# Order of the row gathers, the turn of the next keys and the scaling of the probabilities in a four-layer kernel with paged attention

## The reference, cut to what matters

```python
k_blocks = k_blocks.at[blk, :, off, :].set(k.transpose(0, 2, 1, 3))
v_blocks = v_blocks.at[blk, :, off, :].set(v.transpose(0, 2, 1, 3))
k_all = k_blocks[block_tables].transpose(0, 2, 1, 3, 4).reshape(Bx, G, -1, HD)
v_all = v_blocks[block_tables].transpose(0, 2, 1, 3, 4).reshape(Bx, G, -1, HD)
scores = jnp.einsum('bghtd,bgsd->bghts', qg, k_all) * SCALE
allowed = (kpos[None, None, :] <= pos[:, :, None]) & (kpos[None, None, :] > pos[:, :, None] - WINDOW)
scores = jnp.where(allowed[:, None, None, :, :], scores, -jnp.inf)
p = jax.nn.softmax(scores, axis=-1)
o = jnp.einsum('bghts,bgsd->bghtd', p, v_all).reshape(Bx, H, Tx, HD)
x = x + jnp.einsum('bto,do->btd', o.transpose(0, 2, 1, 3).reshape(Bx, Tx, H * HD), Wo)
```

## Time and profile before

| | |
|---|---|
| median of 3 runs | 185.62 us (184.13 to 185.85) |
| profiled execution | 187.31 us, span 185.5 us |
| granted TensorE clock, mean | 0.844 |
| PE busy, instructions | 125.4 us, 1310 |
| DVE busy | 109.0 us, 404 |
| ACT busy | 77.2 us, 250 |
| POOL busy | 77.0 us, 104 |
| bytes moved | 31.72 MB, mean 171 GB/s |

### The profile page before, as it was taken

The page is one execution under the profiler, slowest core; times in us unless marked ns, Lnnn a source line. Parts: engine busy times, 40 slices in busy tenths (PEclk is TensorE's granted clock), DMA queues, the critical chain, the costliest instruction groups (busy, mean ns, idle before and its releaser), DMA issues.

```text
span 185.5 us, 4024 instructions
## 1 busy us (share of the span) xinstructions
PE 125.4 (68%) x1310; PEld 82.2 (44%) x1310; DVE 109.0 (59%) x404; ACT 77.2 (42%) x250; POOL 77.0 (41%) x104
## 2 busy tenths in 40 slices
PE   0222999910049899040537798988989898999974
PEld 0112955500037487030313343665656565656742
DVE  0886665000099986999111576675888887977220
ACT  0120210005963356992202347583836584763300
POOL 3277640120000123000877888889888740414000
PEclk9999999995557999955555555699999999999999
DMA  4978999999967777671233368852687765465662
GB/s 111 269 159 206 215 146 115 164 200 168 227 187 184 207 189 176 177 236 66 80 92 113 115 189 234 231 179 83 174 266 224 217 179 142 157 166 153 193 173 79
DMA packets 33536, 31.72 MB, mean 171 GB/s; under 512 B 6636, under 2 KB 31340, under 8 KB 32812
## 3 DMA queue, kind: packets, MB, share of 16 engines
q1 hardware_dynamic: 27090, 19.46, 37.7%
q0 software_dynamic: 3216, 11.15, 27.4%
q10 hardware_dynamic: 3210, 0.87, 2.4%
HBM read 23.47 MB, written 8.00 MB: 170 GB/s over the span
## 4 chain that ended last, share of the span: by engine, by line
PE 25%; DMA 20%; SPq 19%; POOL 18%; issue 8%; DVE 6%; ACT 2%; DVEq 0%; POOLq 0%
SPq L342 16%; DMA blk<-in_L_cond_k_blocks,tab_i 14%; POOL kvA L434 8%; PE bank L1157 5%; PE bank L1114 4%; PE bank L1098 4%; DMA kv_rows<-kvn 4%; PE bank L1144 4%; PE bank L1131 3%; SPq L347 3%; PE bank L1152 3%; POOL kvB L427 2%; DMA lens_i<-in_itok_B 2%; POOL tab_i L396 2%; POOL blkp L434 2%
## 5 line engine op out<-in xcount | busy, mean ns | idle before, releaser
L596 ACT ACTIVATE pr<-S,nb 128x160 f32<-128x160 f32 x64 | 26.9, 423 | 17.6 <-DVE nb L906 17.5
L1098 PE MATMUL bank<-KT,QT 32*64 32x160 f32 x256 | 22.5, 374 | 1.2 <-DVE nb L906 0.8
L897 DVE TENSOR_SCALAR pr<-pr,ri 128x128 f32<-128x128 f32 x64 | 21.8, 385 | 1.1
L1017 PE MATMUL bank<-WkvT,x2T 128*128 128x256 f32 x32 | 9.5, 463 | 16.7 <-DVE WqT L775 15.9
L906 DVE CUSTOM_DVE_ANT_0 S<-bank,mask 128x160 f32<-128x160 f32 x64 | 18.1, 319 | 4.5 <-PE bank L1098 4.1
L582 ACT COPY PTA<-bank 128x256 f32<-128x256 f32 x32 | 11.9, 373 | 12.9 <-PE bank L1114 12.8
L434 POOL DMA_INDIRECT kvA<-kv_rows,rowA x16 | 15.4, 961 | 4.5 <-issue 4.5
L434 POOL DMA_INDIRECT blkp<-kv_rows,rowA x16 | 15.7, 983 | 3.2 <-issue 3.0
L1017 PEld LDWEIGHTS bank<-WkvT,x2T 128*128 128x128 f32 x32 | 7.4, 239 | 19.6 <-issue 16.7
L423 POOL TENSOR_TENSOR ksn<-kvn,rot 128x512 f32<-128x512 f32 x2 | 3.5, 1772 | 30.0 <-DVE kvn L823 30.0
L881 DVE COPY KT<-bank 128x512 f32<-128x512 f32 x8 | 5.5, 690 | 16.2 <-PE bank L1076 16.1
(11 more groups left out here) (181 smaller groups left out, 278.1 us busy)
## 6 DMA issues: line engine op xcount, KB each, us to landing
We<-in_L_cond_W SPq DMA_DIRECT2D x16, 256.0 KB, 3.4
kvn<-in_L_cond_W SPq DMA_DIRECT2D x16, 256.0 KB, 3.8
kv_rows<-blkp SPq DMA_DIRECT2D x2, 968.0 KB
xin<-in_x SPq DMA_DIRECT2D x2, 512.0 KB, 8.1
kv_rows<-kvn SPq DMA_DIRECT2D x2, 512.0 KB, 8.3
be<-in_L_cond_b SPq DMA_DIRECT2D x32, 32.0 KB
out<-nat SPq DMA_DIRECT2D x8, 128.0 KB
kv_rows<-QT SPq DMA_DIRECT2D x1, 968.0 KB
```

Source lines behind the costliest of these rows:

```text
L596: act.activation(pr[:, n // B4 % 2, u, n % B4, :], S[:, n % 2, u, :], ACT.Exp, bias=nb[:, n % 4, u:u + 1], scale=-1.0, accum_out=rs[:, n % ...
L897: ts(e_, e_, ri[:, n % 8, u:u + 1], None, ALU.mult).then_inc(s_pn, 1)
L1017: i_ = mm(bank[1 + t // 2][:, (t % 2) * D:(t % 2) * D + D], x2T[:, kc, t * P:(t + 1) * P], WkvT[:, kc, :], start=(kc == 0), stop=(kc == KC ...
L1098: i_ = mm(bank[2 + i % 3][GS * T * k:GS * T * k + GS * T, 0:KEYS], QT[h, g, j, :], KT[h, g % 2, j, :], start=True, stop=True)
```

## The change

The order of the gathers changes, by this part of the diff:

```diff
+FIRST = 4
...
-            for b in range(AHEAD):
+            for b in range(FIRST):
                 gather_a(b)
+            pool.wait_ge(s_kt, 1)
+            nxt = FIRST
             pool.wait_ge(s_cst0, 16)
             for n in range(B + 2):
...
-                if n + AHEAD < B:
-                    gather_a(n + AHEAD)
+                while nxt < min(B, n + AHEAD, 2 * n + FIRST + 2):
+                    gather_a(nxt)
+                    nxt += 1
```

`s_kt` reaches 1 when TensorE has turned the first 128 keys of the first group. After step n the gathers of min(n+10, 2n+6) sequences have been issued; before it was n+11. The turn of the next group's keys stands one step later on TensorE, and so do both copies; each head pair's two products become one:

```diff
# scalar
-                if n % B4 == 1 and n // B4 + 1 < NT:
+                if n % B4 == 2 and n // B4 + 1 < NT:
                     keep_kb(n // B4 + 1)
# vector
-                for u in range(2):
-                    e_ = pr[:, n // B4 % 2, u, n % B4, 0:P]
-                    ts(e_, e_, ri[:, n % 8, u:u + 1], None, ALU.mult).then_inc(s_pn, 1)
+                e_ = pr[:, n // B4 % 2, :, n % B4, 0:P]
+                tt(e_, e_, ri[:, n % 8, :].unsqueeze(2).broadcast_to([P, 2, P]), ALU.mult).then_inc(s_pn, 1)
...
-                if n % B4 == 0 and n // B4 + 1 < NT:
+                if n % B4 == 1 and n // B4 + 1 < NT:
                     keep_k(n // B4 + 1)
# tensor
-                    pe.wait_ge(s_pn, 2 * (B4 * g + j))
+                    pe.wait_ge(s_pn, B4 * g + j)
...
-                if n % B4 == 0 and n // B4 + 1 < NT:
+                if n % B4 == 1 and n // B4 + 1 < NT:
                     turn_ka(n // B4 + 1)
-                if n % B4 == 1 and n // B4 + 1 < NT:
+                if n % B4 == 2 and n // B4 + 1 < NT:
                     turn_kb(n // B4 + 1)
```

## The result

The changed kernel takes 191.08 us, the median of 4 runs (190.06 to 195.32); the kernel before, run beside it, 185.74 (184.13 to 186.44, 4 runs). The ratio is 1.0295, with a 95% interval from 1.0219 to 1.0372: slower by some 5.3 us. The forecast was 190.3 us. (The ratio takes from either kernel only the runs within 1.5% of its fastest; where runs scatter more than that, ratio and medians differ, and I rest on the stages of the traces.) The profiled execution took 191.16 us, its span 189.4, with a mean granted clock of 0.847.

A forecast was written before the change was run, and what follows sets the result against it. GpSimd's queue was taken to bound the kernel up to 121.86 us, TensorE after that. +5.1 (gathers) + 0 (keys' turn) - 0.4 (product) = +4.7 us, 192.0 for the profiled execution, median 190.3 us; range 187.3 to 193.1.

The forecast's parts named there:

- GpSimd's debt: GpSimd's queue up to group 1's turn: four gathers at 1.25 and 0.1 for the start, +5.1 us (+4.7 to +6.0).
- TensorE's readiness: TensorE before group 1's turn: despite late keys of sequences 8 to 11, ready at 127.0, no later than GpSimd; nothing added.
- both turns: Sign: TensorE's turns of groups 0 and 1 at about 118.6 and 127.0, each behind `prB`.
- The turn of the keys one step later: VectorE and TensorE: 2.2 us saved at layer 4, given back before S; 0 us, -0.3 to +0.1 a group.
- The single product: VectorE's one product for two: holdups that lengthen groups can vanish (-0.8) or go on (0); taken as -0.4 us.
- 2 (the clock stays low): TensorE's clock rises only after group 1's turn, +2.8 us, 193.1 us; chance 0.13.
- 3: Rival: the key turn's saving at layer 4 is kept, -2.2 us, 188.1 us; chance 0.15.
- 4: Rival, within 1%: layer 4's saving kept, gathers land at 2.8 (-0.4), no holdups (-0.4), 187.3 us; chance 0.11.
- 5 (the debt costs nothing): Gathers in pairs behind `prB` cost TensorE nothing, its own step sets the pace to 122 us; 182.6 us; chance 0.06.
- both holes: Sign: GpSimd idle twice, 2 us for the turned keys and about 4 us for `ri` of sequence 0.
- the wait for the copied last keys: Sign: TensorE newly waits for the last keys' copy, wanted one step earlier and 0 to 0.3 us late.
- rival 1: The forecast itself: GpSimd's debt stands, the rest cancels; 189.3 to 191.6 us; chance 0.55.

The follow-up runs named there:

- e2: Kernel before with only the new order of gathers (four, the wait for the turned keys, then two per step): 190.68 us, ratio 1.0384.
- e1: Changed kernel with only the order of the gathers undone (ten sequences ahead, then n+10): 188.30 us, ratio 1.0275.
- e4: Changed kernel with eight sequences' gathers issued first instead of four: 185.26 us, ratio 1.0075.
- e3: Changed kernel without GpSimd's wait for the first turned keys: 189.46 us, ratio 1.0263.
- e7: Kernel before with the copy of the keys put behind `x3T` in the same VectorE step: 181.98 us, one run.
- e6: Kernel before with only the single product for two: 186.67 us, one run.
- e11: The kernel of e7 (against the one before) timed again, in a disturbed series: 199.45 us beside 201.06, ratio 0.9754.
- e8: Kernel before with keys' copy behind `x3T`, biases of groups 2 to 7 loaded ahead, nine gathers ahead instead of ten: 182.92 us, ratio 0.9877.
- e10: The kernel of e8 with ten gathers ahead instead of nine, in a disturbed series: 199.85 us beside 202.47, ratio 0.9951.
- e12: The kernel of e8 (against the one before) timed again, in a disturbed series: 196.87 us beside 201.06, ratio 0.9828.

## Why the prediction held, and where it did not

The forecast was 190.3 us, between 187.3 and 193.1, and 191.08 was measured. Stage by stage it is less close: +4.7 us was forecast, and the two traces differ by 6.43, of which 0.98 lies at the end, where the forecast had no term.

**GpSimd's debt: right, +5.09 against +5.1,** but the match to the hundredth is luck, by two errors that cancel. The first `prB` came 0.55 us earlier than before, not 0.1 later, mostly because the gather of sequence 7 landed in 2.69 us, not 3.2. Why it did isn't shown: the gather just ahead of it took 3.77 in e2, whose order is the same. From the first `prB` to the turn of group 1 the sum had four gathers at 1.25, 5.0; the trace has 5.64. The rest is `prB` itself: the first, second and sixth take 0.53, 0.49 and 0.50 us instead of 0.30, 0.62 in all. That the cause is the order of the gathers is shown: from the first gather to the turn of group 1 it takes 34.58 with the order undone (e1), 33.85 with eight first (e4) and 41.15 with the order alone (e2). GpSimd's wait is worth a third of it (37.42 without it, e3). The price of 1.25 a gather stood, and no pair was cheaper.

**TensorE's readiness: right in its result, wrong in its place.** It was counted as never later than GpSimd. In group 0 it was: it stood 2.11 and 1.31 us for the gathers of sequences 10 and 11, while the fourth `prB` was done before the turn. The argument looked at group 1 only. The forecast had both turns behind `prB`. By group 1 `prB` was last again, by 0.18 us, so it cost nothing. In e2 and e3 it was not last: the eighth `prB` had ended 0.7 and 0.5 us before the turn. So the late gathers make two paths of nearly the same length. One is GpSimd's queue, whose gathers stand between the `prB`; the other is the landing of the keys of sequences 8 to 11 and TensorE's steps behind it. The prediction had put both at 127.0 and added nothing for the second.

**The turn of the keys one step later: 0 was too kind.** The mechanism is the one forecast: no wait for `x3T` but the last, and new ones of 0.3 us for S. But a group becomes 9.05 us instead of 8.83, +0.22, where the bounds ended at +0.1. The term that was too small is the wait for S, taken as 0.2 to 0.3 us. The idle time shown is 0.34, but it has to be read from start to start. The scores of one step begin at 132.11 and TensorE's next work at 133.36, 1.25 us later, where an unheld step has 0.43 (130.50 to 130.93): 0.82 lost. The wait for `x3T` is read the same way. In the kernel before, layer 4 at 154.58 starts 0.83 us after the row below; e7 has 0.25 there (147.81 to 148.06): 0.58 saved.

```profile
153.75 0.31 PE L1132 MATMUL bank<-PTB,xin 128*32 128x64 f32 x8
```

The two make +0.24, which accounts for the 0.22. The wait for S is this long because the first keys' copy, the result and S now stand in one step of VectorE:

```profile
131.62 0.69 DVE L885 COPY KT<-bank 128x512 f32<-128x512 f32 x1 [1.92 <-PE bank L1079]
...
132.23 0.41 DVE L938 TENSOR_TENSOR nat<-bank,be 128x256 f32<-128x256 f32 x1
132.56 0.31 DVE L909 CUSTOM_DVE_ANT_0 S<-bank,mask 128x160 f32<-128x160 f32 x1
```

S begins 0.94 us after the copy, and TensorE resumes at 132.94. The groups with a copy of keys were to be 8.8 to 9.0 us; they are 9.05 to 9.33. Over the five groups the changed kernel loses only 0.36, as the kernel before had one group of 9.49 that no later kernel with its keys' turn repeats.

**The single product: no run shows its -0.4.** The five groups take 43.17 us with it alone (e6), but 43.33 with the old pair in e2, so what is missing against the 43.80 of before need not be the product's. It is held up like the pair. VectorE's and GpSimd's rows of the changed kernel, for the earlier trace rows:

```profile
107.50 1.64 DVE L900 TENSOR_TENSOR pr<-pr,ri 128x256 f32<-128x256 f32 x1
...
119.12 0.88 DVE L900 TENSOR_TENSOR pr<-pr,ri 128x256 f32<-128x256 f32 x1
...
126.08 0.42 DVE L900 TENSOR_TENSOR pr<-pr,ri 128x256 f32<-128x256 f32 x1
127.11 1.24 DVE L900 TENSOR_TENSOR pr<-pr,ri 128x256 f32<-128x256 f32 x1
```

```profile
107.80 1.05 POOL L456 TENSOR_TENSOR xin<-kvB,cst 128x512 f32<-128x512 f32 x1
...
118.65 1.06 POOL L456 TENSOR_TENSOR xin<-kvB,cst 128x512 f32<-128x512 f32 x1
...
126.00 0.99 POOL L435 DMA_INDIRECT blkp<-kv_rows,rowA  x1 [0.16 <-issue]
127.01 1.05 POOL L456 TENSOR_TENSOR xin<-kvB,cst 128x512 f32<-128x512 f32 x1
```

Each long product reaches into the spreading on GpSimd and ends some 0.3 us behind it, at 109.14, 120.00 and 128.35. The one at 126.08 lies in a gather and takes 0.42. In this trace and in e6's every product above 0.6 us overlaps a spreading. The pair with a scalar did not mind gathers either: in the kernel before one ran from 107.31 in 0.48 us within the gather 107.14 to 108.13. The prediction took the gather ahead of the spreading in the earlier trace rows for a part of the cause. The Trainium skill (SBUF — State Buffer, "Who interferes with whom") has anything on GpSimd exclude a two-port `tensor_scalar`; the row at 107.31 does not show that for a gather, but no row shows either whether the pair ran in its two-port form. The same section has a product of two tensors held by GpSimd instructions that read SBUF, and this the rows at 107.50 and 127.11 show.

**The end, which no step had.** Behind the last turn 0.98 us more. In the changed kernel the chain of waits runs over SyncE's queue from 174 us on (in e7 from 158), with eight loads a group and at times an issue that takes far longer than 0.38. In the kernel before it stays on TensorE to the end, so SyncE's queue was not last there. The queue's rows of the changed kernel:

```profile
172.71 1.38 SPq L367 DMA_DIRECT2D be<-in_L_cond_b  x1
...
178.68 1.16 SPq L365 DMA_DIRECT2D kvn<-in_L_cond_W  x1
180.03 0.33 SPq L367 DMA_DIRECT2D be<-in_L_cond_b  x1
```

TensorE's last products then waited for the last expert matrix:

```profile
185.62 1.05 PE L1160 MATMUL bank<-kvn,x3T 128*32 128x256 f32 x4 [0.18 <-DMA kvn<-in_L_cond_W]
```

The change doesn't explain it: e4, with the changed kernel's last groups, has 13.62, e2 13.52, e7, with the order, the keys' turn on TensorE and the product of before, 14.92, and e11 16.35. That it is SyncE's bias loads is shown by taking them away: e8, e10 and e12 have 13.45, 13.47 and 13.47, where eleven traces with them scatter from 13.52 to 16.35. (The same edit drops SyncE's wait `s_res` for a result, but the write of that result stands ahead of it in the queue with the same wait, so this changes nothing.)

**The rivals.** 2 (the clock stays low) did not come: the rise is at about 121 us, before the turn of group 1, though it is 2 us later than before, and 4.5 later counted from the first gather. 3 and 4 needed the saving at layer 4 to be kept; it can be, but by e7's order and not by the change's. 5 (the debt costs nothing) falls with e1, e2 and e4. Of the signs named as right, both holes, both turns (31.26 and 39.19 us after the first gather; forecast 30.8 and 39.2), and the new wait came; the wait of group 0's turn for `prB`, the groups of at most 9.0 us and the wait for the copied last keys did not. The range of rival 1 (189.3 to 191.6) held the bounds of the debt and the product but not those of the keys' turn, which for four groups are -1.2 to +0.4.

## What to carry to other kernels

An in-order queue that both starts transfers and computes for the bottleneck should be full of transfers when it has to wait for the first result: count what has been issued by that moment, since every piece issued afterwards stands between two results, here 1.25 us each, and what it brings comes late as well. A producer moved a step later takes its wait along: to take a wait away, change the order within the step (`x3T` ahead of the copy of keys, -0.6 us a group) before moving work over steps. Then see which queue sets the pace next; in e7 it was TensorE, without a wait at 8.24 us a group, with GpSimd's queue at 8.15 just behind, and SyncE's queue in the last two groups.

## What the runs showed of the hardware that was not expected

- GpSimd's `prB` takes 0.53 us instead of 0.30 where it is released together with VectorE's product of two tensors (103.59 beside 103.54, and again in e6), and 0.29 to 0.38 beside the pair with a scalar in the kernel before; over the kernel a mean of 429 ns against 300.
- SyncE's issues of loads take mostly 0.33 to 0.39 us, but up to three of the last 24 take 0.8 to 2.0 us, with no releaser shown.
- Whole series of runs, of every kernel, were 14 to 17.5 us longer with single instructions at their usual length; only their starts were late. Its cause is open.
